# A decoder layer on one core: both chunk inversions on VectorE, six Toeplitz chunks loaded early, group 0's gate walked between the solves

## The chip, the cores and the metric

The kernel runs on one core of a Trainium2 chip. The metric is the device time of one launch in microseconds (us), and lower is better. The five engines each run a program of their own, in order; they meet through semaphores that the code names (`s["..."]`).

## The reference, cut to what matters

The batch is B = 16 sequences of L = 128 tokens, D = 128 columns, H = 4 heads of 32. Three sublayers follow one another, each with a residual and a layer norm.

```python
# sublayer 1: gated delta rule with two FIR branches
q, k, v = (silu(causal_dwconv(x @ W, w_conv)) for W, w_conv in ...)   # 4 taps
beta = sigmoid(x @ Wb)
q, k = l2norm(q), l2norm(k); v = v * beta; kb = k * beta    # chunks of 32 tokens
inv = -(kb @ k.T) * strict_lower            # per head and chunk, 32 x 32
for i in range(1, 32): inv[i, :] += inv[i, :] @ inv         # triangular inverse
u, w = (inv + eye) @ v, (inv + eye) @ kb
for each chunk: ui2 = u - w @ S; o = q @ S + (q @ k.T * lower) @ ui2; S += k.T @ ui2
local_long  = causal_dwconv(v, fir_long)    # 64 taps
local_short = causal_dwconv(v, fir_short)   # 5 taps
stats = head_stats of (local_short, local_long, delta_out, v)   # mean, var, mean |x|, l2
p = clipped softmax(gelu([x, stats] @ Wg1 + bg1) @ Wg2 / temp)
o = p0*short + p1*long + p2*delta + p3*v + gate*short
og = sigmoid(gelu([x, head_stats(o), head_stats(v)] @ Wog1) @ Wog2)
x1 = layernorm(x + rmsnorm(o * og) @ Wo)
# sublayer 2: cross attention on ctx, rotated, with a decay mask, no softmax
x2 = layernorm(x1 + ((rot(x1 @ Wq) @ rot(ctx @ Wk).T) * decay) @ (ctx @ Wv))
# sublayer 3: eight experts (128 -> 256 -> 128), the best two of each token
out = layernorm(x2 + moe(x2))
```

## The kernel before

The sequences are worked in NG = 4 groups of G = 4. The 64 (sequence, head) pairs make two halves, f = 0 and f = 1, of 32 pairs: half 0 is groups 0 and 1, half 1 groups 2 and 3. What follows is in order of time.

**Projections.** `project_step(g)` on TensorE runs the four projections of a group (`project`, L536), the transposes of the scaled keys of the group before (`keys_transposed`), and that group's products of keys with keys and queries (`products`, L563), by halves r = 0 and 1. ScalarE applies silu (`activate`), squares, and copies; VectorE sums the squares and takes roots (`norms`), then masks the products (`mask_products`, L1301). A root is `rsqrt` (L1230): a guess by an integer trick and three Newton steps of three operations, ten in all. Behind group 0's activation ScalarE issues the loads of four Toeplitz chunks (`toeplitz`, L936), each 256 KB, for the long FIR.

**Inversions.** The 32 x 32 triangles go through DRAM to one partition for each (pair, chunk), and come back as `blk[f]`. GpSimd inverts half 0 (L454 to L472), VectorE half 1 (`invert`, L1521), column j = 0 to 30, two operations each. SyncE's queue, written out by hand, has `half_in(1)`, then `inverses_of(0)` (store L365, 16 loads L371), then the context and x of group 0 (L392), then `inverses_of(1)`.

**FIR.** In a loop over CHUNKS = 8 TensorE multiplies v by the Toeplitz chunks (L608) and transposes, with values transposed (`vt_ps`) and the short convolution of one group (L630) in each of four rounds. Chunks 4 to 7 are loaded in this loop, each into the tile of a chunk already used.

**Solves.** For each half, chunks n = 0 to 3: `solve_blocks` (L789) multiplies the inverses by v, ScalarE keeps the result (`keep_solved`, four copies, L1125), `apply_solved` (L775) multiplies it by the key products, and VectorE subtracts (`residual`, L1532). `delta_products` (L796) and `delta_transposed` then make the delta branch of a group, and VectorE scales it (`delta`, L1538). Context work (`ct`, `xat`, `values` L696, `keys` L702) stands between half 0's solves. VectorE sums each branch (`source_sums`, L1367 to L1374) and makes the statistics of it (`source_moments`), first for group 0, then at once for the twelve sequences of groups 1 to 3 (L1352 to L1380).

**Gate of group 0.** VectorE: `source_logits`, `source_weights` (softmax), `mixture`, `mixture_stats`, `gated` (L1433), `x1_norm`. TensorE has the matmuls between: `source_gate`, `st2_transposed`, `output_gate`, `output_z`, `ont`, `wo`.

**Steps 1 to 3.** `step(g)` works the cross attention and the first experts of group g - 1 together with the gate of group g. Step 1 is written out, steps 2 and 3 are a hardware loop, and a tail follows. On VectorE the expert results are added by `add(p, e)` (L1507). GpSimd takes the root of each layer norm (L487) throughout.

## Time and profile before

| | |
|---|---|
| device time, median of 3 runs | 461.27 us (460.3 to 463.18) |
| the profiled execution | 456.92 us, its span 455.2 us |
| granted TensorE clock, mean of the span | 0.865 of full speed |
| busy share of the span | TensorE 75%, VectorE 62%, ScalarE 34%, GpSimd 12% |

The profile is one execution; its durations are those of that run, while the three runs above were taken without a profile. A busy share is an average over stages with different limits, so the stages are read one by one: the chain of waits names what released what, and the timeline of one engine gives start, duration and the idle time before each instruction.

### The profile page before, as it was taken

The page shows a single profiled execution, that of the slowest core. Times are in us where ns is not written, and L with a number is a line of the kernel's source. Part 1 is how long each engine was busy: PE and PEld are TensorE (multiplying, and loading weights), DVE is VectorE, ACT ScalarE, POOL GpSimd, SP SyncE. Part 2 cuts the span into 40 slices and gives each one's busy share as a digit, 9 for nine tenths or more (in the row PEclk, how much of TensorE's full clock was granted, in tenths as well). Part 3 has the DMA queues.
Part 4 walks back from the last instruction along what each step waited for, and adds up shares of the span by engine and source line. Part 5 has one row for each costly group of instructions (what it writes and reads, how often), then busy time and mean ns, then how long its engine had stood idle before and what let it go on. Part 6 is the DMA issues. An engine that isn't in the chain of part 4 may idle for free.

```text
span 455.2 us, 8063 instructions
## 1 busy us (share of the span) xinstructions
PE 340.1 (75%) x2912; PEld 231.7 (51%) x2912; DVE 280.0 (62%) x870; ACT 152.6 (34%) x282; POOL 55.7 (12%) x105
## 2 busy tenths in 40 slices
PE   3809897659995756804255898988889898888993
PEld 1505454338994543602233565665466664665672
DVE  3014655678196675179855766658776688766534
ACT  1312324253535443223011345224343353215240
POOL 6000003898000000000000000100001000000000
PEclk9967999957998675565559799999999999999998
DMA  6293204205954273000010000000200000000000
GB/s 198 50 287 89 49 0 98 41 1 144 273 139 96 70 183 79 3 0 0 1 46 1 23 1 1 23 1 1 71 1 23 0 0 23 0 2 0 25 0 23
DMA packets 52384, 23.53 MB, mean 52 GB/s; under 512 B 18776, under 2 KB 51584, under 8 KB 52352
## 3 DMA queue, kind: packets, MB, share of 16 engines
q1 hardware_dynamic: 35840, 14.71, 12.6%
q10 hardware_dynamic: 16512, 8.39, 7.3%
q8 instruction: 20, 0.33, 0.3%
q14 instruction: 12, 0.10, 0.1%
HBM read 18.77 MB, written 3.28 MB: 48 GB/s over the span
## 4 chain that ended last, share of the span: by engine, by line
issue 49%; PE 21%; DVE 13%; SPq 5%; DMA 5%; ACTq 2%; POOL 2%; ACT 2%; POOLq 0%; DVEq 0%
PE bank L536 6%; PE bank L530 3%; PE bank L563 3%; SPq L359 2%; ACTq L936 2%; POOL sm L487 2%; DMA blocks<-as_t 2%; PE bank L511 2%; SPq L371 2%; DMA wtap<-rbundle 1%; DMA toep<-x 1%; DVE as_t L1507 1%; DVE as_t L1333 1%; DMA inverses<-inv 1%; DVE ss_g L1273 1%
## 5 line engine op out<-in xcount | busy, mean ns | idle before, releaser
L766 PEld LDWEIGHTS bank<-w_sb,as_t 128*128 128x128 f32 x512 | 60.3, 192 | 21.0 <-issue 17.0
L766 PE MATMUL bank<-w_sb,as_t 128*128 128x128 f32 x512 | 63.2, 278 | 5.0 <-ACT as_t L1072 5.0
L1072 ACT ACTIVATE as_t<-bank,cb 128x512 f32<-128x512 f32 x64 | 43.2, 688 | 66.7 <-PE bank L758 51.4
L758 PE MATMUL bank<-as_t,w_sb 128*128 128x512 f32 x128 | 61.9, 608 | 0.0
L1507 DVE SCALAR_TENSOR_TENSOR as_t<-bank,as_t 128x128 f32<-128x128 f32 x128 | 36.1, 345 | 21.7 <-PE bank L766 19.4
L487 POOL TENSOR_TENSOR sm<-sm,neg_half 128x4 f32<-128x4 f32 x12 | 12.1, 1010 | 259.5 <-DVE sm L1329 259.5
L511 PE MATMUL bank<-ident,early 128*128 128x128 f32 x96 | 17.1, 308 | 31.1 <-ACT xc_pad L942 15.8
L536 PE MATMUL bank<-wtap,xc_pad 128*128 128x384 f32 x96 | 36.0, 515 | 0.0
L511 PE MATMUL bank<-ident,as_t 128*128 128x128 f32 (+1 forms) x64 | 11.5, 308 | 32.7 <-issue 13.5
L1301 DVE TENSOR_TENSOR as_t<-bank,masks 128x512 f32 (+1 forms) x32 | 20.1, 691 | 21.4 <-PE bank L563 21.4
L758 PEld LDWEIGHTS bank<-as_t,w_sb 128*128 128x128 f32 x128 | 22.5, 195 | 18.2 <-issue 16.8
L511 PEld LDWEIGHTS bank<-ident,early 128*128 128x128 f32 x96 | 11.7, 154 | 37.8 <-issue 18.5
L536 PEld LDWEIGHTS bank<-wtap,xc_pad 128*128 128x128 f32 x96 | 19.7, 205 | 14.7 <-issue 2.8
L511 PEld LDWEIGHTS bank<-ident,as_t 128*128 128x128 f32 (+1 forms) x64 | 7.2, 141 | 38.8 <-issue 20.7
L466 POOL TENSOR_TENSOR early<-early,inv 128x31 f32<-128x31 f32 (+15 forms) x31 | 16.5, 533 | 69.3 <-DMA early<-blocks 67.0
L1333 DVE TENSOR_SCALAR as_t<-as_t,sm 128x128 f32<-128x128 f32 x48 | 13.4, 344 | 13.5 <-POOL sm L487 13.5
L950 ACT ACTIVATE early<-bank 128x256 f32<-128x256 f32 x16 | 6.2, 385 | 39.5 <-PE bank L536 34.3
L470 POOL TENSOR_TENSOR inv<-inv,early 128x31 f32<-128x31 f32 (+15 forms) x31 | 18.1, 583 | 2.4
L1125 ACT ACTIVATE early<-bank 32x256 f32<-32x256 f32 x32 | 12.0, 375 | 17.7 <-PE bank L789 17.1
L530 PE MATMUL bank<-wtap,xc_pad 128*128 128x392 f32 x32 | 15.4, 565 | 2.7 <-DVE wtap L1251 2.7
L1525 DVE TENSOR_TENSOR wtap<-early,inv 128x31 f32<-128x31 f32 (+15 forms) x31 | 10.7, 345 | 10.7 <-DMA early<-blocks 9.7
L1411 DVE SCALAR_TENSOR_TENSOR as_t<-src,as_t 128x128 f32<-128x128 f32 x48 | 13.8, 348 | 1.1
(225 smaller groups left out, 575.6 us busy)
## 6 DMA issues: line engine op xcount, KB each, us to landing
toep<-taps_back ACTq DMA_DIRECT2D x4, 1024.0 KB, 9.1
w_sb<-taps_back ACTq DMA_DIRECT2D x4, 1024.0 KB, 13.1
toep<-x SPq DMA_DIRECT2D x8, 256.0 KB, 3.0
early<-x SPq DMA_DIRECT2D x4, 256.0 KB, 3.3
blocks<-as_t SPq DMA_DIRECT2D x16, 64.0 KB, 2.2
early<-blocks SPq DMA_DIRECT2D x2, 512.0 KB, 5.9
src<-vb SPq DMA_DIRECT2D x32, 32.0 KB, 3.3
inverses<-inv SPq DMA_DIRECT2D x2, 512.0 KB, 3.6
```

The source lines that it names most:

```text
L466: pool.tensor_tensor(out=p, in0=blk[0][:, j, j + 1:].unsqueeze(1).broadcast_to([128, m, n]), in1=column.unsqueeze(2).broadcast_to([128, m, ...
L470: pool.tensor_tensor(out=rest, in0=rest, in1=p, op=ALU.subtract).then_inc(pool_solve, 1)
L487: pool.tensor_tensor(out=sm2[:, 0:G], in0=sm1[:, 0:G], in1=neg_half[:, :], op=ALU.pow).then_inc(root_done, 1)
L511: last = pe.transpose(ps[dst][0:rows, b * L:(b + 1) * L], source[:, b, :], ident[:, :])
L530: pe.matmul(pr[:, 0:PROJ_W], xc_pad[:, b, PAD:PAD + L], wtap_all[:, (TAPS - 1) * NQKV:TAPS * NQKV + 2 * H], start=True, stop=False)
L536: last = pe.matmul(pr[:, 0:NQKV], xc_pad[:, b, first:first + L], wtap[:, k, :], start=False, stop=(k == 0))
L758: pe.matmul(ps[4 + half][:, :], w1_sb[:, e, half * 128:half * 128 + 128], x2_c.rearrange("p b t -> p (b t)"), start=True, stop=True).then_ ...
L766: last = pe.matmul(bank(6 + e % 2)[:, b, :], hid[:, e % 2, half, b * L:(b + 1) * L], w2_sb[:, e, half, :], start=(half == 0), stop=(half = ...
L1072: act.activation(hid[:, e % 2, half, :], ps[4 + half][:, :], ACT.Relu, bias=c_of("b1", 2 * e + half)).then_inc(s["hid_ready"], 1)
L1301: dve.tensor_tensor(out=rows_of[:, bass.ds(g * G + 2 * r, 2), h, :], in0=bank(4 + h, 2), in1=mid(masks[:, :, :].rearrange("p k t -> p (k t ...
L1333: last = dve.tensor_scalar(dst[:, b, :], y[:, b, :], mv[:, b, 0:1], sm2[:, b:b + 1], ALU.subtract, ALU.mult)
L1507: last = dve.scalar_tensor_tensor(out=acc[:, b, :], in0=bank(6 + e % 2)[:, b, :], scalar=score[:, b, e:e + 1], in1=acc[:, b, :], op0=ALU.m ...
```

## The change

- VectorE inverts both halves. `invert(f, first, last)` runs half 0 as soon as its triangles are in, and half 1 in three pieces, columns 0 to 9, 10 to 15 and 16 to 30, with sums, residuals and deltas between them. GpSimd's inversion is gone, and GpSimd copies each group's v to `src` instead (`v_kept`), since silu now is one operation of 384 columns into `qkv_g`.
- The sums of v move into the projection loop (`square_v`, `v_sums`), and `products(g-1, 1)` behind the last projection, `mask_products(g-1, 1)` behind `norms(g)`. `activate` waits for `vb_ready`, `vsq_ready` and `v_kept`.
- Six Toeplitz chunks are loaded early and have a tile each; 6 and 7 follow in the FIR loop.
- The FIR loop holds the short convolutions of groups 0 and 1 only, group 2's follows, and group 3's stands in quarters between the solves of half 0. The context work of group 0 stands ahead of the first solve.
- `keep_solved` is one copy, from one PSUM tensor of eight banks.
- The gate of group 0 is walked between the solves of half 1. The sums and moments of groups 1 to 3 are made group by group: `three_sums(1)` and its moments in that walk, `three_sums(2)` before step 1, `three_sums(3)` and the moments of groups 2 and 3 inside step 1.
- `rsqrt` has eight operations: a cubic step (four) and a Newton step (three) after the guess.

```diff
-                act.activation(qk_g[:, b, :], pr[:, 0:2 * D], ACT.Silu)
-                act.activation(src[:, bass.ds(g * G + b, 1), 3, :].rearrange("p a c -> p (a c)"), pr[:, 2 * D:3 * D],
-                               ACT.Silu).then_inc(s["silu_ready"], 1)
+                act.activation(qkv_g[:, b, :], pr[:, 0:NQKV], ACT.Silu).then_inc(s["silu_ready"], 1)
...
-            for k in range(4):
+            for k in range(6):
                 toeplitz(k)
...
             def keep_solved(f, n):
                 act.wait_ge(s["d_ps"], f * NC + n + 1)
-                for c in range(4):
-                    first = HP * f + PQ * c
-                    act.activation(u[CH * n:CH * n + CH, first:first + PQ, :],
-                                   ps[c][CH * c:CH * c + CH, 0:PQ * DH].rearrange("p (r d) -> p r d", d=DH), ACT.Copy
-                                   ).then_inc(s["u_ready"], 1)
+                rows = slice(CH * n, CH * n + CH)
+                act.activation(u[rows, HP * f:HP * f + HP, :].rearrange("p (c r) d -> p c (r d)", c=4),
+                               banks[rows, 0:4, 0:PQ * DH], ACT.Copy).then_inc(s["u_ready"], 1)
...
-                for i in range(3):
-                    own(dve.tensor_tensor(out=t, in0=y, in1=y, op=ALU.mult))
-                    own(dve.scalar_tensor_tensor(out=t, in0=t, scalar=-0.5, in1=a, op0=ALU.mult, op1=ALU.mult))
-                    own(dve.scalar_tensor_tensor(out=y, in0=t, scalar=1.5, in1=y, op0=ALU.add, op1=ALU.mult))
+                own(dve.tensor_tensor(out=t, in0=y, in1=y, op=ALU.mult))
+                own(dve.scalar_tensor_tensor(out=t, in0=t, scalar=CUBIC, in1=a, op0=ALU.mult, op1=ALU.mult))
...
+            def three_sums(g):
+
+                dve.wait_ge(s["ssq_ready"], g + 3)
...
-            invert(0, 24)
+            invert(1, 0, 10)
+            source_sums(0, 0, 1)
             residual(0, 1)
-            invert(24, CH - 1)
-            dve.sem_inc(s["solved1"], 1)
+            source_sums(1, G, 2)
             residual(0, 2)
-            sums(0, 0, G, 2)
-            residual(0, 3)
-            sums(1, 0, G, 3)
             dve.wait_ge(w_late, 16 * LATE_LOADS)
             rotate_keys(0)
+            residual(0, 3)
+            invert(1, 10, 16)
             delta(0)
-            source_sums(2, 0, G, 4)
-            residual(1, 1)
+            source_sums(2, 0, 3)
             source_moments(0, G)
-            residual(1, 2)
-            sums(0, G, B, 2)
-            residual(1, 3)
             delta(1)
+            invert(1, 16, CH - 1)
             dve.wait_ge(pool_step, 13)
             source_logits(0)
             source_weights(0)
             mixture(0)
             mixture_stats(0)
+            residual(1, 1)
+            three_sums(1)
+            residual(1, 2)
+            gated(0)
+            source_moments(G, 2 * G)
+            residual(1, 3)
+            x1_norm(0)
             delta(2)
             delta(3)
-            sums(1, G, B, 5)
-            gated(0)
-            source_sums(2, G, B, 6)
-            x1_norm(0)
-            source_moments(G, B)
+            three_sums(2)
...
                 add(p, 2)
+                if not experts_left:
+                    three_sums(3)
+                    source_moments(2 * G, B)
                 gated(g)
```

TensorE around the first solves, before. L789 is `solve_blocks`, L775 `apply_solved`, L511 a transpose (`toep` is here the context), L696 `values`, L702 and L703 `keys`:

```order
L608 MATMUL bank<-w_sb,src 16x128 x16
L511 MATMUL bank<-ident,early 128x128 x8
L789 MATMUL bank<-src,early 32x32 x32
L511 MATMUL bank<-ident,toep 128x128 x8
L775 MATMUL bank<-early,as_t 32x32 x32
L789 MATMUL bank<-src,early 32x32 x32
L696 MATMUL bank<-wb,toep 128x128 x4
L775 MATMUL bank<-early,as_t 32x32 x32
L789 MATMUL bank<-src,early 32x32 x32
L702 MATMUL bank<-toep,wb 128x512
L703 MATMUL bank<-toep,wb 128x512
L775 MATMUL bank<-early,as_t 32x32 x32
```

And now, where they are L796, L782, L502, L703, L709 and L710, and L607 is the short convolution:

```order
L502 MATMUL banks<-ident,early 128x128 x8
L607 MATMUL banks<-diag_short,xc_pad 128x128 x20
L502 MATMUL banks<-ident,toep 128x128 x8
L703 MATMUL banks<-wb,toep 128x128 x4
L709 MATMUL banks<-toep,wb 128x512
L710 MATMUL banks<-toep,wb 128x512
L796 MATMUL banks<-src,early 32x32 x32
L607 MATMUL banks<-diag_short,vc_pad 128x128 x5
L782 MATMUL banks<-early,as_t 32x32 x32
L796 MATMUL banks<-src,early 32x32 x32
L607 MATMUL banks<-diag_short,vc_pad 128x128 x5
L782 MATMUL banks<-early,as_t 32x32 x32
```

The context work has moved ahead of the first solve, and a quarter of group 3's short convolution stands after each solve.

VectorE, before, where the gate of group 0 begins (L1386, `source_logits`), after the sums of twelve sequences and the last two deltas that come ahead of it:

```order
L1380 TENSOR_TENSOR st_all<-st_all,stat_scale 128x64
L1532 TENSOR_TENSOR src<-src,bank 128x2x128
L1367 TENSOR_REDUCE sumx<-src 128x12x4
L1369 TENSOR_REDUCE sumq<-sq_g 128x12x4
L1372 TENSOR_REDUCE st_all<-src 128x12
L1374 TENSOR_REDUCE st_all<-sumx 128x12
L1532 TENSOR_TENSOR src<-src,bank 128x2x128
L1538 TENSOR_TENSOR src<-bank,rq 128x4x128
L1386 SCALAR_TENSOR_TENSOR as_t<-bank,temp,bg_t 128x16
L1388 TENSOR_REDUCE as_t<-as_t 128x4
```

And now, from the end of group 0's moments, over the inversion of half 1 (columns 16 to 30), to the logits (L1450):

```order
L1406 TENSOR_REDUCE st_all<-wtap 128x16
L1444 TENSOR_TENSOR st_all<-st_all,stat_scale 128x64
L1600 TENSOR_TENSOR src<-banks,rq 128x4x128
L1585 TENSOR_TENSOR wtap<-early,inv 128x255
L1587 TENSOR_TENSOR inv<-inv,wtap 128x17x15
...
L1587 TENSOR_TENSOR inv<-inv,wtap 128x29x3
L1585 TENSOR_TENSOR wtap<-early,inv 128x60
L1587 TENSOR_TENSOR inv<-inv,wtap 128x30x2
L1585 TENSOR_TENSOR wtap<-early,inv 128x31
L1587 TENSOR_TENSOR inv<-inv,wtap 128x31
L1450 SCALAR_TENSOR_TENSOR as_t<-banks,temp,bg_t 128x16
```

The last fifteen columns of half 1 now stand directly ahead of the logits of group 0; the sums of the other groups are behind them.

VectorE in step 1, before, between the third `add` and `gated` (L1433):

```order
L1452 TENSOR_TENSOR toep<-bank,tab 128x512
L1453 TENSOR_TENSOR toep<-bank,tab 128x512
L1454 TENSOR_TENSOR toep<-toep 128x512
L1507 SCALAR_TENSOR_TENSOR as_t<-bank,as_t 128x128 x4
L1433 TENSOR_SCALAR as_t<-as_t 128x4
L1434 TENSOR_TENSOR sm<-as_t 128x4
L1435 TENSOR_TENSOR as_t<-nt,sm 128x16
```

And now (L1518 ends `rotate_keys`, L1571 is `add`, L1497 begins `gated`):

```order
L1517 TENSOR_TENSOR toep<-banks,tab 128x512
L1518 TENSOR_TENSOR toep<-toep 128x512
L1571 SCALAR_TENSOR_TENSOR as_t<-banks,as_t 128x128 x4
L1431 TENSOR_REDUCE sumx<-src 128x4x12
L1433 TENSOR_REDUCE sumq<-sq_g 128x4x12
L1436 TENSOR_REDUCE st_all<-src 128x4x3
L1437 TENSOR_REDUCE st_all<-sumx 128x4x3
L1400 TENSOR_TENSOR wtap<-sumx 128x128
L1401 SCALAR_TENSOR_TENSOR wtap<-sumq,wtap 128x128
...
L1406 TENSOR_REDUCE st_all<-wtap 128x32
L1444 TENSOR_TENSOR st_all<-st_all,stat_scale 128x128
L1497 TENSOR_SCALAR as_t<-as_t 128x4
```

Four reductions of four sequences by three branches and fifteen operations of 128 columns have come in ahead of `gated`.

## Rows read from the trace of the kernel before

**Rows 1.** The page: TensorE's granted clock in 40 slices.

```profile
PEclk9967999957998675565559799999999999999998
```

**Rows 2.** Chain of waits in time order: start us, us, what; ScalarE's queue.

```profile
22.90 5.00 ACTq L936
...
27.93 3.56 ACTq L936
```

**Rows 3.** The same chain in the projection loop.

```profile
66.47 1.95 PE bank L536 x6
...
78.66 1.08 PE bank L563 x16
...
84.46 1.95 PE bank L536 x6
```

**Rows 4.** Timeline of VectorE, norms of groups 2 and 3: start us, us, instruction.

```profile
73.39 0.19 DVE L1235 SCALAR_TENSOR_TENSOR nt<-nt,ss_g 128x32 f32<-128x32 f32 x1
...
92.87 0.55 DVE L1235 SCALAR_TENSOR_TENSOR nt<-nt,ss_g 128x32 f32<-128x32 f32 x1
```

**Rows 5.** Timeline of VectorE: the last masked products.

```profile
103.83 2.71 DVE L1301 TENSOR_TENSOR as_t<-bank,masks 128x512 f32<-128x512 f32 x4 [1.33 <-PE bank L563]
```

**Rows 6.** Windows of VectorE: us, busy (x), granted clock, DMA share, GB/s.

```profile
124.20:143.60 19.40, 17.71 (x48) 1.00 0.58 138
146.70:151.10 4.40, 3.92 (x15) 0.50 0.02 6
```

**Rows 7.** Timeline of SyncE's DMA queue.

```profile
128.06 0.35 SPq L365 DMA_DIRECT2D inverses<-inv  x1
...
139.70 0.45 SPq L392 DMA_DIRECT2D toep<-ctx_in  x1
```

**Rows 8.** Timeline of TensorE, 140 to 162 us.

```profile
140.32 0.75 PE L789 MATMUL bank<-src,early 32*32 32x32 f32 x64 [0.71 <-ACT src L1104]
...
143.31 0.66 PE L511 MATMUL bank<-ident,toep 128*128 128x128 f32 x4 [2.24 <-DMA toep<-ctx_in]
...
152.80 2.08 PE L702 MATMUL bank<-toep,wb 128*128 128x512 f32 x2
...
159.53 1.96 PE L796 MATMUL bank<-as_t,early 128*32 128x128 f32 x64 [1.67 <-ACT early L1125]
```

**Rows 9.** Groups by line, shapes apart: busy us, mean ns | idle before.

```profile
L1372 DVE TENSOR_REDUCE st_all<-src 128x12 f32<-128x1536 f32 x3 | 5.3, 1754 | 0.1
...
L958 ACT ACTIVATE sq_g<-early 128x1024 f32<-128x1024 f32 x3 | 3.2, 1058 | 0.0
...
L1235 DVE SCALAR_TENSOR_TENSOR wtap<-wtap 128x192 f32<-128x192 f32 x3 | 1.1, 358 | 0.1
```

**Rows 10.** Timelines of VectorE and TensorE, inversion columns to step 1.

```profile
136.68 0.43 DVE L1525 TENSOR_TENSOR wtap<-early,inv 128x255 f32<-128x255 f32 x1
...
166.43 0.22 DVE L1352 TENSOR_TENSOR wtap<-sumx 128x64 f32<-128x64 f32 x1
...
170.38 0.22 DVE L1380 TENSOR_TENSOR st_all<-st_all,stat_scale 128x64 f32<-128x64 f32 x1
...
194.65 0.17 DVE L1395 TENSOR_REDUCE as_t<-as_t 128x4 f32<-128x16 f32 x1 [9.69 <-ACT as_t L1020]
...
227.84 1.09 PE L511 MATMUL bank<-ident,as_t 128*128 128x128 f32 x4 [6.17 <-DVE as_t L1333]
```

**Rows 11.** Timelines of VectorE and TensorE in step 1.

```profile
238.70 0.69 DVE L1458 TENSOR_TENSOR as_t<-bank,tab 128x512 f32<-128x512 f32 x1 [4.90 <-PE bank L714]
...
278.95 0.17 DVE L1433 TENSOR_SCALAR as_t<-as_t 128x4 f32<-128x4 f32 x1 [0.22 <-ACT as_t L1037]
...
282.82 0.66 PE L511 MATMUL bank<-ident,as_t 128*128 128x128 f32 x4 [0.57 <-DVE as_t L1441]
...
290.45 0.60 PE L511 MATMUL bank<-ident,as_t 128*128 128x128 f32 x4
```

**Rows 12.** A window: busy of PE, PEld, DVE, ACT, POOL (x), then granted clock, DMA share, GB/s.

```profile
235.00:240.00 5.00, 5.00 (x8) 1.71 (x6) 1.26 (x2) 0.59 (x1) 0.00 (x0) 0.50 0.00 0
```

More of the change, by code:

```diff
@@ L231, in decoder_kernel @@
         x_in = sem("x_in")
-        toep_in = [sem(f"toep_in{k}") for k in range(4)]
+        toep_in = [sem(f"toep_in{k}") for k in range(8)]
         blocks_out = sem("blocks_out")
@@ L596, in _, with values_transposed, short_conv @@
             pe.wait_ge(s["dve_const"], 1)
+            def values_transposed(g):
+                if g >= 2:
+                    pe.wait_ge(s["vc_ready"], g - 1)
+                transposes(4 + g % 2, src[:, g * G:g * G + G, 3, :]).then_inc(s["vt_ps"], 1)
+            def short_conv(g, b):
+                bank_of = (6, 7, 6, 5)[g]
+                if b == 0:
+                    pe.wait_ge(s["vc_ready"], NG if g == 3 else g + 1)
+                    if g == 2:
+                        pe.wait_ge(s["short_ready"], 1)
+                    if g == 3:
+                        pe.wait_ge(s["vh_ready"], 1)
+                for i in range(SHORT):
+                    last = pe.matmul(bank(bank_of)[:, b, :], v_columns[g % 2][:, b, i:i + L],
+                                     diag_short[:, i, :], start=(i == 0), stop=(i == SHORT - 1))
+                return last
             for k in range(CHUNKS + 1):
                 if k < CHUNKS:
-                    pe.wait_ge(toep_in[k % 4], 16 * (k // 4 + 1))
+                    pe.wait_ge(toep_in[k], 16)
                     if k >= 2:
@@ L788, in solve_blocks @@
                         rows = slice(CH * c, CH * c + CH)
-                        last = pe.matmul(ps[c][rows, r * DH:(r + 1) * DH], inv_t[rows, f, n, r, :],
+                        last = pe.matmul(ps[c][CH * n:CH * n + CH, r * DH:(r + 1) * DH], inv_t[rows, f, n, r, :],
                                          vs[rows, f, n, r // H, r % H * DH:(r % H + 1) * DH],
@@ L944, in activate @@
             def activate(g, b):
-                act.wait_ge(s["k_ready"], g)
-                act.wait_ge(s["tanh_ready"], g)
+                act.wait_ge(s["vb_ready"], g + credit["vb_ready"])
+                act.wait_ge(s["vsq_ready"], g)
+                act.wait_ge(s["v_kept"], g + credit["v_kept"])
                 act.wait_ge(s["q_ps"], g + credit["q_ps"])
@@ L1131, in keep_delta @@
                 act.activation(o_c[:, g, :, :], bank(O_BANKS[g]), ACT.Copy).then_inc(s["oc_ready"], 1)
[L1133 to L1142 removed]
+            for n in range(NC):
+                keep_solved(0, n)
             act.wait_ge(inverse_out[0], 16)
+            keep_short(3)
             keep_delta(0)
@@ L1267, in gate_sums, with v_sums @@
                                   op=ALU.add).then_inc(s["zsum_ready"], 1)
+            def v_sums(g):
+                seqs = bass.ds(g * G, G)
+                dve.wait_ge(s["vsq_ready"], g + 1)
+                dve.wait_ge(s["v_kept"], g + 1 + credit["v_kept"])
+                rows = src[:, seqs, 3, :]
+                own(dve.tensor_reduce(out=sumx[:, seqs, 3, :], in_=rows.rearrange("p n (h d) -> p n h d", h=H),
+                                      axis=AX.X, op=ALU.add))
+                own(dve.tensor_reduce(out=sumq[:, seqs, 3, :],
+                                      in_=sq_g[:, 2 * G:3 * G, :].rearrange("p n (h d) -> p n h d", h=H),
+                                      axis=AX.X, op=ALU.add))
+                dve.tensor_reduce(out=st_all[:, seqs, 14], in_=rows, axis=AX.X, op=ALU.add,
+                                  apply_absolute_value=True)
+                dve.tensor_reduce(out=st_all[:, seqs, 12], in_=sumx[:, seqs, 3, :], axis=AX.X, op=ALU.add)
+                dve.sem_inc(s["vsums_ready"], 1)
             def norms(g):
@@ L1515, in finish, with invert @@
                 layernorm(acc, fin, "fin_ready")
-            def sums(k, a, b, squares_ready):
-                source_sums(k, a, b, squares_ready)
-                dve.sem_inc(s["sums_ready"], 1)
-            def invert(first, last):
+            def invert(f, first, last):
                 for j in range(first, last):
@@ L1541, in delta @@
                                   ).then_inc(s["delta_ready"], 1)
-            sums(3, 0, B, 1)
+            dve.wait_ge(blocks_in[0], 16)
+            invert(0, 0, CH - 1)
+            v_sums(NG - 1)
             dve.wait_ge(s["act_const"], 1)
```

296 lines of the change are left out of this document (161 added, 135 removed).

## The prediction

> **What bounds the kernel now.** I read the page's shares first, then the chain of waits in order of time, then the timeline of each stage. TensorE is busy 75% of the span, but unevenly, and its granted clock is at half in two places, near 25 us and between 140 and 245 us [rows 1]. So three stretches are limited by something else. (a) At 21 to 33 us ScalarE hands over four Toeplitz loads; the third and fourth issue hold it 5.00 and 3.56 us, and the squares and copies that feed the next projections stand behind them [rows 2]. (b) In the projection loop one group takes 18.0 us (the last projections end at 68.4 and 86.4), in a ring: last projection, squares, VectorE's norms, transposes of the scaled keys, next projections [rows 3]. (c) From 106 to 234 us the chain goes through the inversions, the solves and then VectorE alone: sums, mixture, gate, layer norm. From there on TensorE is the bound, with VectorE close behind it.
>
> **Toeplitz issues, +7.1.** Six are issued early instead of four, and group 1's copies and the first squares, which began when the fourth ended (31.5), wait for them [rows 2]. By the fourth, the last whose issue was held up, each costs 3.56: 2 x 3.56 = 7.1 us. Bounds: 0.8 (two issues like those of SyncE that stand below, 0.35 to 0.45) and 10.0 (2 x 5.00). I take 3.56, since the queue is full by then. The Trainium skill, "DMA: Bandwidth & Descriptors", Issuing engines are not separate DMA queues, says that the time to initiate a DMA is usually small beside the DMA itself; by that this term would be near its lower bound, and the two rows of 5.00 and 3.56 contradict it here.
>
> **Projection loop, -4.1.** products(g-1, 1), 16 matmuls that the chain shows with 1.08 us together, moves behind the last projection of a group and so out of the ring [rows 3]; that is -1.1 for each of groups 1, 2 and 3. Each root loses two of ten operations, 0.23 us apart [rows 4]: -0.45 in groups 2 and 3. Together -3.3 - 0.9 = -4.2, say -4.1. The added waits of activate (vb_ready, v_kept, vsq_ready) hold ScalarE some 1.4 us longer, and behind them the key copies; TensorE then has the second projection before it, so I price them at nothing. Without that cover they cost up to 1.4 x 3 = 4 us. GpSimd's new copy of v runs while VectorE waits for the squares, and v_sums (estimate 2.2 us a group) lies in VectorE's idle time.
>
> **Tail of the projections, -3.1.** In the norms of the last group VectorE's 32-column operations take 0.55 us where they took 0.19 in the group before [rows 4]. What differs is that GpSimd is then in its inversion. That inversion goes, so 2.6 us (six slowed operations and the key product) and one root's 0.45 come back. The Trainium skill, "SBUF — State Buffer", Who interferes with whom, says that a VectorE instruction with two SBUF inputs contends with a GpSimd instruction that reads SBUF; the 0.55 against 0.19 agrees. Sum so far 7.1 - 4.1 - 3.1 = -0.1: VectorE has masked its last products at 106.4 instead of 106.5 [rows 5].
>
> **Inversions, one after the other on VectorE.** Half 1 took VectorE 19.4 + 4.4 us less some edges, 23.6 [rows 6]. Now half 0 needs that first: 106.4 + 23.6 = 130.0. SyncE stored half 0 at 128.06 and issued the context load at 139.70, so this comes 1.9 later, at 141.6 [rows 7]. TensorE has lost one of four short convolutions there and waits for the load from about 136. The first solve now stands behind ct, xat, values and keys: context at 145.2 (143.31 less 139.70 is 3.6), two transposes 2.2 (twice the 1.09 of four at the slow clock, below), keys 3.3 (their first pair 2.08, the second faster), values 2.1 like that pair, copies of 0.7: first solve at 153.7, before at 140.3 [rows 8]. In return a round of the solve is shorter: one ScalarE copy of 1024 columns (estimate 1.05, from the squares of that size [rows 9]) instead of four, and nothing but a quarter of a short convolution beside it. Solve 0.75, copy 1.05, apply 0.76, residual 0.42 and handoffs 0.3 make 3.3 us, against 4.8 to 5.3. 153.7 + 3 x 3.3 + 0.75 + 1.2 = 165.6 for delta_products, before 159.5 [rows 8]: **+6.1**.
>
> **Group 0 among the solves of half 1.** VectorE has inverted columns 0 to 9 and summed by 141 and then idles for the residual, which is behind 21 columns in need of it but ahead in the queue. Residual 3 ends at 163.6; columns 16 to 30 take 11.2 (before, column 16 began at 136.68, 12.5 after half 1's start, of 23.6 [rows 10]), and columns 10 to 15, two operations of 0.43 and the pauses, 5.5. So 163.6 + 5.5 + delta 0.7 + square 0.7 + sums 2.2 + moments 3.7 (4.2 from 166.43 to 170.60 less two operations of 0.23 [rows 10]) + delta 0.7 + 11.2 = 188.3. Here the logits, the softmax and the mixture of group 0 are queued behind the inversion; TensorE has the logits at about 184. The weights start at 189.3, before at 194.65: still -5.3 [rows 10]. From there to TensorE's start of step 1 at 227.84 it was 33.2 us [rows 10]. In that stretch one three-row sum goes (3 x 1.75 + 0.2 = 5.4 [rows 9]) and four root operations (0.8); one set of moments (3.7) and three residuals (1.3) come; three waits come: the square of the mixture behind keep_solved(1, 0), which waits for the inverse stored at 188.4 (2.6), gated for a tanh that now stands behind a solve (1.3), and residual 3 for an apply behind wo (1.3). Behind x1_norm there is now a tail: solve, copy, delta products at the slow clock (3.6), transposes, deltas; 4.0 more than x1_norm gives, less the 1.3 of deltas that were inside. 33.2 - 5.4 - 0.8 + 3.7 + 1.3 + 5.2 + 4.0 - 1.3 = 39.9. Step 1 starts at 229.2, before at 227.8: **+1.4**.
>
> **Step 1 of the mixing.** Before, moments for three groups kept rotate_queries until 238.70. Now three_sums(2) does: x1 transposes and copy 1.8, square 1.5, sums 5.4, so 238.0, **-0.7**. The large term is further on. three_sums(3) and the moments of two groups are queued on VectorE between add(0, 2) and gated(1). gated began at 278.95, 0.22 after VectorE became idle, so nothing covers them [rows 11]. TensorE can do result 3 and hidden 5, as before, and then stands before ont(1), whose wait at 282.82 was 0.57. Price: 5.4 for the sums and 15 operations of 128 columns, 0.325 apart (estimate between the 0.26 of 64 columns [rows 10] and 0.39 of 192, which last 0.358 [rows 9]) = 4.9, together **+10.3**, less one root 0.4. Ten us of idle will take the clock down, as after the gaps before 240, where it stands at 0.50 [rows 12]: ont, wo, hidden 6 and two results, 7.6 us from 282.82 until the next x1 transposes at 290.45, then lose about **3** (bounds 0 and 7.6). Steps 2 and 3 get back two roots each where VectorE leads, 4 x 0.42 = **-1.7**.
>
> **Sum**, against the profiled execution: +1.4 turned to -0.7 at the queries, +10.3 - 0.4 + 3 - 1.7 = **+10.5**. It took 456.9 us in all, the median of the unprofiled runs is 461.3, 4.4 more. The difference goes on the median: 461.3 + 10.5, I say **471**. One per cent, 4.6 us, is about what a measurement of this kernel can tell from no change.
>
> **Rivals.**
> 1. *The Toeplitz issues cost little.* If the queue takes all six, 0.8 instead of 7.1: 465. For it: the first two issues were free. Against: the third and fourth were not. By the skill's sentence on issuing time quoted above this is the case. Chance 0.12.
> 2. *The clock holds.* Short convolutions, context work and gates fill TensorE between 145 and 228 us. If it is granted full speed there instead of 0.5, the pieces of matmul on the path (gates, logits, output gate, z, ont, wo, delta products and transposes of groups 2 and 3, about 22 us at the slow clock) halve: -11; and the 3 of step 1 stay away if its gap is seen as short: 471 - 14 = 457, with half 0's solve faster still (2 us) 455, over 1% **faster** than before. It decides from a granted clock of some 0.9 in that stretch on. Against: the path waits there for VectorE, and TensorE's share of work was low between 195 and 235. Chance 0.10. The Trainium skill, "TensorE: Matmul & The Clock Gate", What's actually happening, has the throttled state as the default that activity releases; so more work on TensorE is what this case would need.
> 3. *The added waits bite.* activate behind vb_ready delays the key copies so that the loop stays at 18 us: +4 to +5, 476. Chance 0.15.
> 4. *No net change*: the stall in step 1 is partly filled, or the tail of the projections gives more than 3: 459 to 465. Chance 0.18.
> The forecast itself, 466 to 475, has 0.45.
>
> **How the numbers follow.** Faster needs under 456.7: rival 2 and an edge of 4, 0.13. Within 1% (456.7 to 465.9): rival 1 in part, most of 4, 0.24. Slower the rest, 0.63. The range takes in rival 3 with the upper bounds of the issues and the clock term, and rivals 1 and 4: **458 to 482**.
>
> **What would show it.** ScalarE held some 39 us instead of 31.5 before its first squares; groups 16.5 us apart; solved0 at about 130; VectorE idle for over 10 us before the first residual; step 1's x1 transposes within 3 us of 228; TensorE idle for about 10 us before ont(1) behind VectorE's sums and moments. If that last gap is missing, or the clock is full in 145 to 228, the prediction is wrong.

## The result, and the profile after

The changed kernel takes 483.6 us (median of four runs, 478.4 to 486.8; the kernel before 461.8). Two of the four took 486.7 us at a lower granted clock (0.828, the others 0.840 and 0.846) and are left out of every comparison, as such runs of the kernels below are. The other two, 478.4 and 480.5, give a ratio to the kernel before of 1.038, with a 95% interval of 1.031 to 1.045. The times below compare the profile of 480.5 us (span 478.5) with that of before (span 455.2). The two profiled runs are 23.6 us apart (480.5 and 456.9), while 479.5 and 461.8, the times that are compared, are 17.7 apart. So some 6 us of what the stages add up to below belong to the choice of runs.

The page of the changed kernel: the span, the busy shares, the granted clock in 40 slices, and the packets that bring instructions.

```profile
span 478.5 us, 8067 instructions
PE 350.5 (73%) x2912; PEld 241.4 (50%) x2912; DVE 296.3 (62%) x931; ACT 147.9 (31%) x246; POOL 23.5 (5%) x47
...
PEclk9956999859975985555856996998999699999998
...
q14 instruction: 17, 0.14, 0.1%
```

VectorE has 16 us more work than before, GpSimd 32 less. The clock row has two new low places, slices 25 (step 1, the 6 behind 6 9 9) and 32 (the 6 behind 8 9 9 9), and the low stretch ahead of step 1's experts lasts longer: it is at 0.50 from 240 to 250 us, where the kernel before had 0.99.

The way along the chain, in milestones:

| us from the start | before | forecast | after |
|---|---|---|---|
| ScalarE has issued the early Toeplitz loads | 31.5 | 39 | 40.05 |
| VectorE has masked the last products | 106.5 | 106.4 | 106.5 |
| first solve of half 0 | 140.3 | 153.7 | 153.8 |
| delta products of group 0 | 159.5 | 165.6 | 169.7 |
| group 0's weights | 194.65 | 189.3 | 193.55 |
| x1 transposes of step 1 | 227.8 | 229.2 | 231.5 |
| x1 transposes of step 2 | 290.45 | 302.7 | 305.8 |
| end of the span | 455.2 | 465.7 | 478.5 |

First the chain of waits on ScalarE's queue, which answers to [rows 2]: start, us, what.

```profile
22.96 1.44 ACTq L944
...
24.43 4.85 ACTq L944
...
29.32 3.56 ACTq L944
...
32.90 3.56 ACTq L944
...
36.49 3.56 ACTq L944
```

From the third of these rows on each issue costs 3.56 us, so two more cost 7.1. (The profile has 1024 KB for each of these loads, not the 256 KB of the section on the kernel before.) Then VectorE (timeline): a 32-column operation of the last group's root, and the last masked products.

```profile
92.95 0.19 DVE L1263 SCALAR_TENSOR_TENSOR nt<-nt 128x32 f32<-128x32 f32 x1
...
103.80 2.71 DVE L1348 TENSOR_TENSOR as_t<-banks,masks 128x512 f32<-128x512 f32 x4 [1.33 <-PE banks L554]
```

The 0.55 us of [rows 4] is 0.19 in this kernel, where GpSimd doesn't invert, and the end of the projections is where it was [rows 5]. TensorE (timeline) from the context to half 0's delta products:

```profile
145.44 2.12 PE L502 MATMUL banks<-ident,toep 128*128 128x128 f32 x8 [11.57 <-DMA toep<-ctx_in]
...
153.76 1.03 PE L796 MATMUL banks<-src,early 32*32 32x32 f32 x64
...
157.40 0.74 PE L796 MATMUL banks<-src,early 32*32 32x32 f32 x64 [0.61 <-DVE src L1594]
...
161.23 0.26 PE L782 MATMUL banks<-early,as_t 64*32 64x32 f32 x6 [1.14 <-issue]
...
166.07 0.33 PE L782 MATMUL banks<-early,as_t 96*32 96x32 f32 x16 [1.36 <-issue]
167.04 0.74 PE L796 MATMUL banks<-src,early 32*32 32x32 f32 x64 [0.64 <-DVE src L1594]
...
169.69 2.90 PE L803 MATMUL banks<-as_t,early 128*32 128x128 f32 x64
```

It waits 11.57 us for the context. The solves stand at 153.76, 157.40, 162.1 and 167.04; the second and third round took 4.7 and 4.9 us where I had 3.3. One reason stands in the rows of 161.23 and 166.07: 1.14 and 1.36 us with the cause "issue" in the middle of an apply (L782), 2.5 of the 4.1 us by which delta products are later than forecast. Then VectorE's weights, and TensorE's x1 transposes of step 1, output transposes, and x1 transposes of step 2.

```profile
193.55 0.17 DVE L1459 TENSOR_REDUCE as_t<-as_t 128x4 f32<-128x16 f32 x1 [0.28 <-ACT as_t L1034]
```

```profile
231.46 0.66 PE L502 MATMUL banks<-ident,as_t 128*128 128x128 f32 x4 [0.81 <-DVE src L1600]
...
295.93 1.11 PE L502 MATMUL banks<-ident,as_t 128*128 128x128 f32 x4 [10.06 <-DVE as_t L1505]
...
305.77 0.60 PE L502 MATMUL banks<-ident,as_t 128*128 128x128 f32 x4
```

The wait of 0.57 us ahead of the output transposes [rows 11] has become 10.06. VectorE shows what it waits for: sums of group 3, moments (up to L1444), and only then the gate (L1497).

```profile
282.39 1.75 DVE L1431 TENSOR_REDUCE sumx<-src 128x48 f32<-128x1536 f32 x1
...
292.03 0.29 DVE L1444 TENSOR_TENSOR st_all<-st_all,stat_scale 128x128 f32<-128x128 f32 x1
292.48 0.17 DVE L1497 TENSOR_SCALAR as_t<-as_t 128x4 f32<-128x4 f32 x1 [0.15 <-DVE st_all L1444]
```

All this was forecast within 2.5 us a stage, but for the solves. The largest thing that was not forecast is between steps 2 and 3. VectorE at the start of step 3, the first adds (L1571):

```profile
360.14 1.11 DVE L1571 SCALAR_TENSOR_TENSOR as_t<-banks,as_t 128x128 f32<-128x128 f32 x4
365.89 0.35 DVE L1571 SCALAR_TENSOR_TENSOR as_t<-banks,as_t 128x128 f32<-128x128 f32 x1 [4.64 <-issue]
368.09 0.87 DVE L1571 SCALAR_TENSOR_TENSOR as_t<-banks,as_t 128x128 f32<-128x128 f32 x3 [1.85 <-issue]
```

And the same place in the kernel before, which had no such idle:

```profile
345.31 1.12 DVE L1507 SCALAR_TENSOR_TENSOR as_t<-bank,as_t 128x128 f32<-128x128 f32 x4
346.94 1.13 DVE L1507 SCALAR_TENSOR_TENSOR as_t<-bank,as_t 128x128 f32<-128x128 f32 x4 [0.52 <-DVE as_t L1507]
349.10 0.69 DVE L1458 TENSOR_TENSOR as_t<-bank,tab 128x512 f32<-128x512 f32 x1 [1.03 <-PE bank L714]
```

VectorE stands still for 4.64 and 1.85 us and waits for no semaphore. The DMA view of 355 to 372 us has four packets of instructions just there, and the windows of TensorE (us, busy, clock, DMA share, GB/s) show what it costs behind it.

```profile
q14 instruction: 4, 0.03, 0.9%
```

```profile
360.00:365.00 5.00, 5.00 (x26) 1.00 0.20 56
365.00:370.00 5.00, 0.73 (x2) 0.96 0.01 3
370.00:375.00 5.00, 3.81 (x17) 0.50 0.00 0
375.00:380.00 5.00, 5.00 (x18) 0.51 0.00 0
```

TensorE runs dry from 365.7 to 371.2 us, and its clock falls to half for the next ten. From the x1 transposes to the context transposes, step 3 takes 27.7 us instead of 18.6: 9.1 us that no term of mine had. The 50 us behind the start of step 3 (360.6 to 410.6) have five packets of that queue, 8 KB each:

```profile
q14 instruction: 5, 0.04, 0.4%
```

In the kernel before, the 50 us behind the start of its step 3 (346 to 396) have none. There the second pass of the loop brought in no instructions in that time; here it did, and two of the five packets arrive while VectorE stands still for the first time.

### The profile page after: what moved, and what is told of

Read it like the earlier page. It is cut to its first block, busy times and chain, and to the rows that moved or that the text cites. A ratio compares the mean times of both kernels' runs of the same rounds, so it can differ in the third digit from the quotient of the medians.

```text
span 478.5 us, 8067 instructions
## 1 busy us (share of the span) xinstructions
PE 350.5 (73%) x2912; PEld 241.4 (50%) x2912; DVE 296.3 (62%) x931; ACT 147.9 (31%) x246; POOL 23.5 (5%) x47
## 3 DMA queue, kind: packets, MB, share of 16 engines
q1 hardware_dynamic: 35840, 14.71, 12.2%
## 4 chain that ended last, share of the span: by engine, by line
issue 40%; PE 25%; DVE 20%; ACTq 4%; DMA 3%; ACT 3%; SPq 2%; POOL 2%; POOLq 0%; DVEq 0%
PE banks L527 7%; ACTq L944 4%; DVE inv L1587 3%; DVE wtap L1585 3%; PE banks L502 3%; PE banks L521 3%; PE banks L554 2%; SPq L372 2%; POOL sm L477 2%; DMA inverses<-inv 1%; PE banks L796 1%; PE banks L803 1%; PE banks L607 1%; DMA wtap<-rbundle 1%; PE banks L782 1%
## 5 line engine op out<-in xcount | busy, mean ns | idle before, releaser
L773 PEld LDWEIGHTS banks<-w_sb,as_t 128*128 128x128 f32 x512 | 61.9, 196 | 22.0 <-issue 17.7
L773 PE MATMUL banks<-w_sb,as_t 128*128 128x128 f32 x512 | 64.8, 282 | 5.0 <-ACT as_t L1086 5.0
L1086 ACT ACTIVATE as_t<-banks,cb 128x512 f32<-128x512 f32 x64 | 43.2, 686 | 78.7 <-PE banks L765 61.6
L765 PE MATMUL banks<-as_t,w_sb 128*128 128x512 f32 x128 | 63.6, 622 | 0.0
L1571 DVE SCALAR_TENSOR_TENSOR as_t<-banks,as_t 128x128 f32<-128x128 f32 x128 | 36.0, 343 | 31.0 <-PE banks L773 22.7
L502 PE MATMUL banks<-ident,early 128*128 128x128 f32 x96 | 16.9, 307 | 30.1 <-ACT xc_pad L950 20.8
L527 PE MATMUL banks<-wtap,xc_pad 128*128 128x384 f32 x96 | 36.2, 517 | 0.0
L765 PEld LDWEIGHTS banks<-as_t,w_sb 128*128 128x128 f32 x128 | 23.3, 201 | 19.0 <-issue 17.6
L502 PE MATMUL banks<-ident,as_t 128*128 128x128 f32 (+1 forms) x64 | 11.9, 316 | 24.0 <-DVE as_t L1505 12.5
L502 PEld LDWEIGHTS banks<-ident,early 128*128 128x128 f32 x96 | 11.5, 153 | 35.5 <-issue 23.5
L527 PEld LDWEIGHTS banks<-wtap,xc_pad 128*128 128x128 f32 x96 | 19.6, 205 | 14.8 <-issue 3.1
L1348 DVE TENSOR_TENSOR as_t<-banks,masks 128x512 f32 (+1 forms) x32 | 20.1, 688 | 11.1 <-PE banks L554 11.1
L1587 DVE TENSOR_TENSOR inv<-inv,wtap 128x31 f32<-128x31 f32 (+15 forms) x62 | 21.6, 348 | 2.1
L502 PEld LDWEIGHTS banks<-ident,as_t 128*128 128x128 f32 (+1 forms) x64 | 7.6, 146 | 30.0 <-DVE as_t L1505 15.1
L1381 DVE TENSOR_SCALAR as_t<-as_t,sm 128x128 f32<-128x128 f32 x48 | 13.4, 342 | 13.5 <-POOL sm L477 13.5
L796 PE MATMUL banks<-src,early 32*32 32x32 f32 x512 | 7.8, 220 | 10.6 <-DMA early<-inverses 7.6
## 6 DMA issues: line engine op xcount, KB each, us to landing
toep<-taps_back ACTq DMA_DIRECT2D x4, 1024.0 KB, 11.2
```

Source lines behind the costliest of these rows:

```text
L502: last = pe.transpose(ps[dst][0:rows, b * L:(b + 1) * L], source[:, b, :], ident[:, :])
L527: last = pe.matmul(pr[:, 0:NQKV], xc_pad[:, b, first:first + L], wtap[:, k, :], start=False, stop=(k == 0))
L765: pe.matmul(ps[4 + half][:, :], w1_sb[:, e, half * 128:half * 128 + 128], x2_c.rearrange("p b t -> p (b t)"), start=True, stop=True).then_ ...
L773: last = pe.matmul(bank(6 + e % 2)[:, b, :], hid[:, e % 2, half, b * L:(b + 1) * L], w2_sb[:, e, half, :], start=(half == 0), stop=(half = ...
L1086: act.activation(hid[:, e % 2, half, :], ps[4 + half][:, :], ACT.Relu, bias=c_of("b1", 2 * e + half)).then_inc(s["hid_ready"], 1)
L1348: dve.tensor_tensor(out=rows_of[:, bass.ds(g * G + 2 * r, 2), h, :], in0=bank(4 + h, 2), in1=mid(masks[:, :, :].rearrange("p k t -> p (k t ...
```

## The experiments

Ten kernels ran, in three sets; each was compared with the kernel before on the same chip (462 us). "The changed kernel" is 479.5 us below, the mean of the two runs that are compared. Where a gain is followed from stage to stage, keep in mind that traces differ without a cause in the edit: the two kernels that only add empty increments (below) reach step 1 4.7 and 2.7 us ahead of the changed kernel.

### Kernel before, roots of eight operations

```diff
 def rsqrt(y, a, t):        # in the kernel before
-    3 x (multiply, multiply by a, step)
+    the cubic step and one Newton step of the changed kernel
```

> The kernel before with the eight-operation roots alone. By the terms of the prediction the roots give back 0.9 us in the projection loop, 0.5 in group 0's moments, 0.8 up to step 1 and 1.7 in steps 2 and 3: about 457 to 458 us. In the changed kernel VectorE stood still for 6.5 us between steps 2 and 3 with the cause 'issue' (not seen in the kernel before), and instruction packets were fetched just then. Rival: the shorter loop body alone brings that stall; then the time is 461 to 466 us, and the profile shows VectorE idle for 4 us or more at the first adds of step 3.

455.1 us, ratio 0.985 (0.980 to 0.990). By the medians the roots alone are worth 7 us (interval 4.6 to 9.2), where I summed 4. The two profiles differ by 1.2 us only (spans 454.0 and 455.2; the profiled run of the kernel before was a fast one, 456.9 against 462), so they don't show where the rest lies. The profile shows no stall between steps 2 and 3. The shorter body by itself isn't the cause.

### Late sums left out

```diff
 add(p, 2)
-if not experts_left: three_sums(3); source_moments(2 * G, B)
+if not experts_left: dve.sem_inc(s["stats_ready"], 1)
```

> The changed kernel without the sums of group 3 and the moments of groups 2 and 3 in step 1 (their statistics are left at 1, so this part of the computation is left out). My term: 10.3 us of VectorE work plus some 3 us of lowered clock, so 13 us less than the changed kernel, 466 to 470 us. Rival, that other work fills the gap: 5 us less or none. The stall between steps 2 and 3 stays in either case if it is a matter of code fetching, and goes if it is a consequence of the late start of the statistics.

This kernel leaves out the sums of group 3 and the moments of groups 2 and 3. 456.6 us, 23 less instead of 13. The ten that are too many are the stall: with 20 instructions less ahead of the loop it is gone (idle for "issue" between steps 2 and 3: none; 12 packets of instructions instead of 17), and step 3 takes 54.1 us instead of 63.4. At the x1 transposes of step 2 the kernel is 13.4 us ahead (292.4 against 305.8), but 1.9 of that it had at those of step 1 (229.6 against 231.5), ahead of the piece that was taken out. Step 1 itself is 11.5 shorter, against a term of 13.

### VectorE's steps 2 and 3 written out

```diff
-with dve.Fori(2, NG) as g:
+for g in range(2, NG):
```

> The changed kernel with VectorE's steps 2 and 3 written out instead of looped. Theory: the 6.5 us of idle VectorE between steps 2 and 3 are the fetch of the loop's first instructions after the jump back; without a jump they go, and the clock stays up: 8 us less, 470 to 474 us. Rival: the fetch comes late wherever the code goes on, so straight code stalls as well, 478 to 487 us.

468.4 us (466.9 to 469.1), 11 less, somewhat below the 470 that I expected. The stall is gone: by the profile 9.1 us come back in the first part of step 3. Ahead of step 2 the kernel is 2.7 us earlier and in step 2 1.0 faster, and for these I have no cause. The rival, that straight code stalls as well, fell too. The profile does have VectorE idle for "issue" at x1_norm (L1511) in each step, 1.6 to 3.0 us, but this is no stall: the add begins 0.1 us behind TensorE's output matmuls (L691), for which the code waits, and the looped kernels have it too. In the changed kernel, TensorE, then VectorE:

```profile
297.73 2.07 PE L691 MATMUL banks<-wo_n,as_t 128*128 128x128 f32 x8 [0.69 <-ACT as_t L1055]
```

```profile
299.90 0.69 DVE L1511 TENSOR_TENSOR as_t<-banks,toep 128x512 f32<-128x512 f32 x1 [2.99 <-issue]
```

So "issue" alone doesn't name a stall. Between steps 2 and 3 it does, since what VectorE needs there is ready: TensorE's last results ended at 360.7 us, and VectorE stood from 361.25 to 365.89.

### Context ahead of the inverses

```diff
+sp.wait_ge(s["fir_ps"], CHUNKS); the loads of context and x of group 0
 inverses_of(0)
-sp.wait_ge(s["fir_ps"], CHUNKS); the loads of context and x of group 0
```

> The changed kernel with SyncE's three loads of context and x ahead of the store and the 16 loads of half 0's inverses. The first solve then stands behind the inverse loads alone and starts at about 144.5 us instead of 153.8: my reading of the 11.6 us wait of TensorE for the context says -9 at the first solve. VectorE then inverts half 1 (columns 10 to 30) earlier by as much, so the time is 469 to 473 us. Rival: what follows is bound by VectorE's inversion, so that less than 4 of the 9 us reach the end.

470.0 us, 9.5 less (465.7 to 470.1). TensorE (timeline), context transposes, first solve, the second round's apply and the delta products:

```profile
135.81 0.60 PE L502 MATMUL banks<-ident,toep 128*128 128x128 f32 x4
...
141.55 0.75 PE L796 MATMUL banks<-src,early 32*32 32x32 f32 x64
...
148.76 0.26 PE L782 MATMUL banks<-early,as_t 64*32 64x32 f32 x6 [1.07 <-issue]
...
156.29 2.35 PE L803 MATMUL banks<-as_t,early 128*32 128x128 f32 x64
```

The context work now ends at 141.6 and the first solve is 12.2 us earlier; 13.8 us of gain stand at step 1 and 11.1 at step 2. The rival, that VectorE's inversion holds the rest back, fell. The apply waits 1.07 us for "issue" here as well, behind the same matmul as in the row of 161.23, 12 us earlier. Six more of the kernels of this section show it there (0.69 to 1.04 us), so this stall follows the code, not the time.

### Four Toeplitz loads early

```diff
-for k in range(6): toeplitz(k)
+for k in range(4): toeplitz(k)
...
-if k in (2, 3): toeplitz(k + 4)
+if k < 4: toeplitz(k + 4)
```

> The changed kernel with four Toeplitz loads early and the other four in the first four rounds of the FIR loop, as before the change. Two issues of 3.56 us leave ScalarE's queue ahead of group 1's copies. My term says -7.1 at the end of the projections, and since half 0's inversion and the context behind it hang on that end, also at the first solve: 472 us (the changed kernel's undisturbed runs are 478.4 and 480.5). Rival: the loads in the FIR loop come late or the end is bound elsewhere, so that under 3 us reach the end: 476 to 480.

474.3 us (473.4 to 475.3), 5 less. VectorE's last masked products:

```profile
97.14 2.70 DVE L1348 TENSOR_TENSOR as_t<-banks,masks 128x512 f32<-128x512 f32 x4 [1.33 <-PE banks L554]
```

They end at 99.84 instead of 106.5, 6.7 us earlier, so the term of 7.1 was right; 5.3 of it are left at the end of the span. The loads in the FIR loop came in time, since TensorE never waits for one. But two of their issues hold ScalarE for 3.9 and 3.7 us there too, TensorE waits 2.60 us for a copy behind the first of them, and the first solve is 5.7 us earlier instead of 6.7.

### The loop moved by 108 and by 54 instructions

```diff
 source_sums(0, 0, 1)
+for _ in range(108):          # 54 in the other kernel
+    dve.sem_inc(unused, 1)
 residual(0, 1)
```

> The changed kernel with 108 empty semaphore increments on VectorE, put where it waits 14 us for the first residual, so that they cost nothing by themselves. They only move the code of the loop of steps 2 and 3 further on. The kernel without the late sums had 20 instructions less ahead of the loop, the same loop, and no stall between steps 2 and 3. Theory A, the stall depends on where the loop stands against the pieces in which code is fetched, in pieces of 128: 108 more is the same place as 20 less, the stall is gone, 469 to 472 us. Theory B, it depends on how much code there is: the stall stays, 478 to 487 us.

471.0 us (469.8 to 471.6), 8.5 less for 108 instructions more; step 3 takes 54.1 us instead of 63.4. VectorE at the start of step 3:

```profile
359.00 1.11 DVE L1572 SCALAR_TENSOR_TENSOR as_t<-banks,as_t 128x128 f32<-128x128 f32 x4
360.65 1.13 DVE L1572 SCALAR_TENSOR_TENSOR as_t<-banks,as_t 128x128 f32<-128x128 f32 x4 [0.54 <-DVE as_t L1572]
362.78 0.69 DVE L1523 TENSOR_TENSOR as_t<-banks,tab 128x512 f32<-128x512 f32 x1 [1.00 <-PE banks L722]
```

> The changed kernel with 54 empty increments in place of 108: VectorE's loop then begins at instruction 630 of 1009. If the stall repeats with a period of 128 instructions, this is the same place as 502, where the kernel before has its loop (498) and no stall: 469 to 472 us. If the stall belongs to all positions past some length of code, 108 would have shown it; if it belongs to a broad band of positions around 576, it is here too: 478 or more.

470.9 us (469.9 to 471.3): no stall either. So neither the length of the code nor a broad band around 576 makes it. Counted in VectorE's instructions of the built program, waits and register operations too, the loop begins at 684 and 630 here, at 576 in the changed kernel. These counts come from the program, not from a trace. A period of 128 agrees with all runs but isn't shown: by it 684 is 556, where the kernel without the late sums had its loop, and 630 is 502, near the 498 of the kernel before. In neither kernel does a packet of instructions arrive in the 50 us behind the start of step 3.

### The kernel before, its loop moved to the changed kernel's place

```diff
 # kernel before, eight-operation roots
+for _ in range(97):
+    dve.sem_inc(unused, 1)
 dve.wait_ge(blocks_in[1], 16)
```

> The kernel before with eight-operation roots (455.1 us) and 97 empty semaphore increments on VectorE, where it waits 9.7 us for half 1's triangles. The loop of steps 2 and 3 then stands at the very instruction numbers of the changed kernel (575 to 834 of 955), with nothing else of the change. Theory (position of the loop): the stall between steps 2 and 3 appears here too, 4 to 7 us of idle VectorE there and 461 to 465 us. Rival (the stall comes of the changed kernel's schedule or its DMA traffic): 455 to 457 us and no such idle.

468.7 us (466.9 to 471.5) against 455.1 without the 97: 13.5 us, more than the 6 to 10 that I expected, for instructions that do nothing, in a place where VectorE waits anyway (half 1's inversion begins at 122.8 us, without them at 122.3). VectorE's first adds of step 3, and the packets of instructions in the page:

```profile
346.29 0.35 DVE L1513 SCALAR_TENSOR_TENSOR as_t<-bank,as_t 128x128 f32<-128x128 f32 x1 [4.79 <-issue]
348.51 0.87 DVE L1513 SCALAR_TENSOR_TENSOR as_t<-bank,as_t 128x128 f32<-128x128 f32 x3 [1.88 <-issue]
```

```profile
q14 instruction: 17, 0.14, 0.1%
```

The same two idle times as in the changed kernel, 4.79 and 1.88 us, and the same 17 packets. Nothing of the change is needed for the stall but the position of the loop. The two profiles are 10.8 us apart (spans 464.8 and 454.0). From the x1 to the x2 transposes of step 3 the one with the increments takes 8.9 us longer; what follows is 5.4 longer, with a clock of 0.74 from 385 to 405 us, where the kernel without the increments had 1.00 from 380 to 400; and step 3 began 3.5 earlier. Why these last two is open.

### Late sums spread over VectorE's waits

```diff
 rotate_queries(p)
+three_sums_part(3, 0)
 decay_scores(p)
 source_logits(g)
+three_sums_part(3, 1)
 x2_norm(p)
 source_weights(g)
+three_sums_part(3, 2)
 route_max(p)
...
 mixture_stats(g)
+source_moments(2 * G, B)
 start_sum(p)
...
 add(p, 2)
-three_sums(3)
-source_moments(2 * G, B)
```

> The changed kernel with group 3's sums and the moments of groups 2 and 3 spread in step 1 over places where VectorE waits for TensorE (ahead of the decay, the norm, the routing and the start of the sum) instead of in one piece ahead of the gate. If it is the place that costs, most of the 13 us come back: 467 to 470 us, with TensorE's 10 us gap ahead of the output gate's matmuls gone. Rival: VectorE is full in step 1, so the 10 us only move: 476 or more. The loop stands at the same instruction numbers as in the changed kernel, so by the theory of position its stall stays.

470.9 us (470.5 to 472.0), 8.6 less, just above the 467 to 470 expected. TensorE's output transposes and x1 transposes of step 2:

```profile
285.86 0.66 PE L502 MATMUL banks<-ident,as_t 128*128 128x128 f32 x4 [0.16 <-DVE as_t L1523]
...
293.49 0.60 PE L502 MATMUL banks<-ident,as_t 128*128 128x128 f32 x4
```

The gap of 10.06 us is 0.16, and the transposes stand at 293.49 instead of 305.77. The work is the same; its place in VectorE's queue was the cost. Of these 12.3 us 2.7 went again in step 2 (57.4 us instead of 54.8, the clock at 0.66 from 300 to 305). The stall between steps 2 and 3 stayed (4.5 and 1.9 us), as it should at the same position.

### All four together

```diff
+ the edits of the four kernels above: loads of context, Toeplitz, sums, 108 increments
```

> The changed kernel with the four mendings that the runs so far tell apart: four Toeplitz loads early (measured -5 at the end), context loads ahead of the inverses (-10), late sums spread (-9), and 108 empty increments that move the loop (-8.5). If they add up on the changed kernel's 479.5 us: 447 us, 3% under the kernel before and under the kernel before with eight-operation roots (455). Rival: they overlap, since each shortens the wait of the same chain (the first two both pull the first solve), and the inversions on VectorE become the bound: 452 to 458.

448.1 us, ratio 0.971 (0.967 to 0.974): 3% under the kernel before. The four gains, 9.5, 5.2, 8.6 and 8.5, add up to within 1 us. But one of the edits now costs time by itself. TensorE's first solve, first apply and second solve of half 0,

```profile
135.23 0.75 PE L797 MATMUL banks<-src,early 32*32 32x32 f32 x64
...
137.23 0.75 PE L783 MATMUL banks<-early,as_t 32*32 32x32 f32 x64
145.32 1.36 PE L797 MATMUL banks<-src,early 32*32 32x32 f32 x64 [7.34 <-DVE src L1613]
```

are the three rows; the third waits 7.34 us for VectorE's residual, and VectorE has this:

```profile
144.76 0.42 DVE L1613 TENSOR_TENSOR src<-src,banks 128x256 f32<-128x256 f32 x1 [9.76 <-issue]
```

The ten columns of half 1 and the sums ended at 135.0 us, the apply at 138.0, and the residual begins at 144.8. In between stand only the 108 increments. Alone they fitted into VectorE's wait of 14.2 us ahead of this residual; here the wait has shrunk to some 3 us, and they take 9.8. So the rival (VectorE's inversions as the bound) isn't what these rows show: the increments delay the first residual by an estimated 6.7 us (144.8 against 138.1). No run has them in another place, so what that would give at the end is open.

## Why the prediction was right, and where it was short

- **Forecast against result.** 471 forecast (461.3 + 10.5 is 471.8), slower by 2.1%; measured 479.5, 3.8%: 17.7 us where I had 10.5. The range ended at 482: the two runs that are compared lie in it, the median of all four, 483.6, is 1.6 above. Sign and stages were right. That the miss was 8.5 us is in part luck: against the profiles it is 12.8 us of span (465.7 forecast, 478.5), 9.7 of them behind the start of step 2, 0.8 in step 1 and 2.3 ahead of it. The forecast took its differences from one profile and added them to a median 4.4 us above it, and that hid some of the miss.
- **Toeplitz issues, +7.1.** Right: two more issues of 3.56, and 6.7 us at the end of the projections when they are taken away. Rival 1 fell. The Trainium skill, "DMA: Bandwidth & Descriptors", Issuing engines are not separate DMA queues, calls the time to initiate a DMA usually small relative to the DMA itself. Here an issue of 1 MB held ScalarE for 3.56 us, where the load took 11.2 from issue to landing: a third, and not small. That the queue was full, which was my reason for 3.56, no run shows.
- **Projection loop and its tail, -7.2.** Right. The last projections of groups 1 to 3 are 16.2 us apart (forecast 16.5, before 18.0), the 0.55 us operations are at 0.19, and the sum of the three terms came out at 106.5. Their parts were +6.3 at group 1's last projection, -3.6 in the loop and -2.7 behind it, so that small misses cancelled. Rival 3, the added waits, fell with it.
- **Inversions in a row, first solve 153.7.** Right to 0.1 us (the terms as written add up to 153.5), with the context loads issued 0.7 later and the wait for them as named.
- **"A round of the solve ... 3.3 us": mis-sized.** It was 3.6, 4.7 and 4.9; the delta products came at 169.7, 10.2 later than before instead of 6.1. Of each of the two longer rounds 1.1 to 1.4 us is TensorE idle for "issue". The kernel before has such an idle too, 2.01 us in the second apply of half 1. That this is code being fetched is argued only: two packets of instructions of another queue (q8, 16 KB each) arrive from 158 to 167 us, and a round is 138 matmuls by the profile in under 5 us, but no run changes it.
- **Group 0 among the solves, +1.4.** The 4.1 us were carried along (weights at 193.55, forecast 189.3), and 2.0 came back up to step 1: 37.9 us instead of 39.9. The three waits, forecast at 2.6, 1.3 and 1.3, were 2.2, 1.4 and 1.4. Measured +3.6.
- **Step 1, -0.7 and +10.3, +3.** The queries came at 239.5, forecast 238.0. The piece ahead of the gate, forecast at 9.9 with 3 for the clock, was 11.5 by the kernel without it and 12.0 by the kernel that spreads it, each counted from step 1 on. Right. Missing was a term behind the queries: up to the x2 transposes it took 14.3 us instead of 11.4, with TensorE at 0.50 instead of 0.99 from 240 to 250. It is hidden in the sum, since the other parts came out smaller; the clock behind the gap, for one, cost 2.2 instead of 3.
- **"Steps 2 and 3 get back two roots each where VectorE leads, 4 x 0.42 = -1.7": the step that failed.** Step 2 gave 0.5. Step 3 lost 9.1 in its first part and 8.4 in all: VectorE had to fetch the loop's first instructions after the jump back (packets of instructions arrive in its idle time, and only in the kernels that stall), TensorE ran dry for 5.5 us and then ran at half clock. The kernel before with a moved loop shows the same, the changed kernel with a moved or written-out loop doesn't. I priced what the loop's instructions do, never where they stand.
- **Rival 2, the clock holds.** It fell: between 194 and 230 us the granted clock was 0.50 (before 0.53), though 0.93 instead of 0.82 from 154 to 170.
- **Rival 4, no net change.** It fell: the gap in step 1 was 10.06 us, and the tail of the projections gave 2.7.
- **Open.** Why the loop at 576 to 834 stalls and five other places don't (a period of 128 is only consistent), and what TensorE's idle in the applies is.

## What to carry to other kernels

Ahead of a hardware loop on a tuned kernel, count instructions: look at the loop's second pass for idle time with the cause "issue" beside packets of instructions, and move the loop with empty increments in a wait before judging an edit by its total. The increments take time themselves, 9.8 us for 108, and must be looked at again when the wait that hides them shrinks. A block of work on a side engine is priced by who stands behind it in that queue; the same ten us of sums cost 12 us of step 1 in one piece and nothing there in four. And loads that are needed next belong ahead of those that will be waited for anyway: moving three loads gave 10 us.

## What the hardware showed that I had not expected

- A jump back in a loop of 258 VectorE instructions cost 4.1 to 4.8 and 1.8 to 1.9 us in the five kernels that had it at instructions 576 to 834, with 17 instead of 12 or 13 packets of instructions in the profile; it cost nothing at the starts 480, 498, 556, 630 and 684 (four bodies of 258 and one of 266). In the 50 us behind the start of step 3 the five have five packets each, the six other looped kernels none: where the loop doesn't stall, its second pass brings in no instructions in that time.
- The idle time behind it is worth more than itself: TensorE's granted clock, 1.00 from 360 to 365 us, was 0.50 from 370 to 375, and step 3 lost 9.1 us for 6.5 of VectorE's idle.
- Two operations less in each root were worth 7 us (4.6 to 9.2) in the whole kernel, where the parts on the path that I could see made 4.
- Empty semaphore increments on VectorE are not free: an estimated 0.09 us each, from 9.76 us for 108 in the combined kernel.
